# Spreading the rough score pieces of the first attention over other steps, in a macaron network on one Trainium2 core

## What is computed

```python
q, k, v = (heads(x @ W) for W in (Wq, Wk, Wv))       # 16 heads of 16
scores = jnp.einsum('bthd,bshd->bhts', q, k) * tril  # a later key counts as score 0
attn = softmax(scores / T ** 0.5)
out = jnp.einsum('bhts,bshd->bthd', attn, v) @ Wo
```

## Time and profile before

| | us |
|---|---|
| median of 3 runs | 2254.46 (2253.89 to 2258.62) |
| the profiled execution | 2254.67 |
| its span, first to last instruction | 2252.9 |
| TensorE busy in the span | 2004.6 (89%) |
| VectorE busy | 1301.1 (58%) |
| ScalarE busy | 785.7 |
| GpSimd busy | 866.8 |

### The profile page before, as it was taken

The page is one execution under the profiler, slowest core; times in us unless marked ns, Lnnn a source line. Parts: engine busy times, 40 slices in busy tenths (PEclk is TensorE's granted clock), DMA queues, the critical chain, the costliest instruction groups (busy, mean ns, idle before and its releaser), DMA issues. The chain is left out here.

```text
span 2252.9 us, 29291 instructions
## 1 busy us (share of the span) xinstructions
PE 2004.6 (89%) x8700; PEld 1245.8 (55%) x8701; DVE 1301.1 (58%) x2970; ACT 785.7 (35%) x1293; POOL 866.8 (38%) x684
## 2 busy tenths in 40 slices
PE   5899868889888799967599999999899999999987
PEld 5566635545554666646455555555565555555456
DVE  7322275777785722237466666666656666666525
ACT  1122244555555122223223333333413333433323
POOL 0344301231112044432026555556425555565632
PEclk9999969999999599988579999999999999999999
DMA  9111132331220811132331122122122222211101
GB/s 380 47 63 58 54 122 29 42 44 29 29 29 7 341 56 60 61 103 109 73 69 42 46 56 50 38 54 56 22 63 57 57 52 56 56 45 42 31 0 50
DMA packets 60569, 150.62 MB, mean 67 GB/s; under 512 B 12977, under 2 KB 18305, under 8 KB 58177
## 3 DMA queue, kind: packets, MB, share of 16 engines
q1 hardware_dynamic: 50208, 120.43, 20.4%
q0 software_dynamic: 9120, 24.92, 3.5%
q10 hardware_dynamic: 1152, 4.19, 0.5%
HBM read 68.95 MB, written 18.61 MB: 39 GB/s over the span
## 5 line engine op out<-in xcount | busy, mean ns | idle before, releaser
L1831 POOL TENSOR_TENSOR mla_PS<-mla_PS,mla_PT 128x1024 f32<-128x1024 f32 x192 | 457.7, 2384 | 222.2 <-ACT mla_PT L2110 219.6
L2253 DVE TENSOR_REDUCE mla_MXP<-PS 128x1 f32<-128x512 f32 x512 | 343.3, 689 | 241.9 <-PE PS L1910 236.6
L2110 ACT ACTIVATE mla_PT<-PS 128x1024 f32<-128x1024 f32 x256 | 262.4, 1026 | 401.9 <-PE PS L1929 399.5
L1938 PE MATMUL PS<-mla_PT,mla_CN 128*64 128x512 f32 x1024 | 275.3, 616 | 0.1
L1910 PE MATMUL PS<-mla_KH,mla_QH 113*128 113x512 f32 x512 | 216.6, 459 | 30.1 <-DMA mla_KL<-mla_SL 18.8
L521 DVE COPY moe_HT<-PS 128x512 f32<-128x512 f32 x92 | 63.6, 692 | 306.9 <-PE PS L644 301.0
L1929 PE MATMUL PS<-mla_QH,mla_KH 113*128 113x512 f32 x512 | 211.3, 413 | 1.0 <-ACT mla_QH L2097 1.0
L675 POOL DMA_INDIRECT moe_XS<-rows_in,moe_GI x96 | 93.5, 974 | 307.1 <-PE PS L630 171.7
L1929 PE MATMUL PS<-mla_QL,mla_KH 113*128 113x512 f32 x512 | 202.2, 395 | 0.0
L1929 PE MATMUL PS<-mla_QH,mla_KL 113*128 113x512 f32 x512 | 201.3, 393 | 0.0
L1910 PEld LDWEIGHTS PS<-mla_KH,mla_QH 113*128 113x128 f32 x512 | 90.7, 193 | 192.0 <-DVE mla_MXP L2253 123.5
(11 more groups left out here) (297 smaller groups left out, 3203.2 us busy)
## 6 DMA issues: line engine op xcount, KB each, us to landing
W<-in_W_dram SPq DMA_DIRECT2D x16, 2048.0 KB, 28.1
mla_QH<-mla_SH SPq DMA_DIRECT2D x64, 128.0 KB, 2.4
mla_KH<-mla_SH SPq DMA_DIRECT2D x64, 128.0 KB, 2.4
mla_QL<-mla_SL SPq DMA_DIRECT2D x64, 128.0 KB, 2.5
mla_KL<-mla_SL SPq DMA_DIRECT2D x64, 128.0 KB, 2.4
mla_KH<-mla_SH SPq DMA_DIRECT2D x64, 96.0 KB, 2.4
mla_KL<-mla_SL SPq DMA_DIRECT2D x64, 96.0 KB, 2.4
sums_Y<-rows_out SPq DMA_DIRECT2D x9, 512.0 KB, 6.1
```

The costliest lines, as they stand in the source:

```text
L1831: pool.tensor_tensor(PS[:, :], PT[:, slot(0), :] if k == 1 else PS[:, :], PT[:, slot(k), :], ALU.add).then_inc(s_ps.handle, 1)
L1938: ins = pe.matmul(bank(6)[h * DKVL:(h + 1) * DKVL, :], CN[:, b, k, 0:DKVL], PT[:, slot(k), h * HB:(h + 1) * HB], start=(k == 0), stop=(k = ...
L2110: act.activation(PT[:, slot(k), :], banks(st_bank(s, 0), 2)[:, :], ACT.Exp, scale=MLA_SCALE).then_inc(s_p.handle, 1)
L2253: dve.tensor_reduce(MXP[:, n // NPC, c, h, t:t + 1], bank(piece_bank(n))[:, :], AX_X, ALU.max).then_inc(s_mx.handle, 1)
```

## The change

It alters two tables. `per_slot` says how many rough pieces a slot does. Before: 2 in slots 8 to 11, 1 in slots 12 to 15, 2 in slots 16 to 23 and 2 in slots 0 to 5 of the next group. After: 2 in each slot from 8 to 23, 2 in slots 0 to 2, 1 in slots 3 and 4 and none in slot 5. So 32 pieces, not 28, are done by the end of slot 23, and before slot 0 of group 0. The assertion is loosened to match. `FILL` moves the filler of slot 6 to slot 7; every group has one there.

```diff
-    per_slot = {s: 2 for s in range(FROM, NSL)} | {s: 1 for s in range(FROM + 4, FROM + 8)} | {s: 2 for s in range(6)}
-    assert sum(per_slot.values()) == NPC and sum(per_slot[s] for s in range(FROM, FROM + 8)) == NPC0
+    per_slot = {s: 2 for s in range(FROM, NSL)} | {0: 2, 1: 2, 2: 2, 3: 1, 4: 1}
+    assert sum(per_slot.values()) == NPC and sum(per_slot[s] for s in range(FROM, FROM + 8)) >= NPC0
...
-    FILL = (3, 6, 9, 13, 15, 22)
+    FILL = (3, 7, 9, 13, 15, 22)
```

## The result

The changed kernel takes 2265.9 us (median of 5 runs, 2264.79 to 2267.84) against 2254.96 (5 runs) for the kernel before: a ratio of 1.0051, with a 95% interval of 1.0041 to 1.0062. It is slower by 10.9 us. The forecast was 2264. The profiled execution's span went from 2252.9 to 2264.6. Two single executions further down, one of the kernel before (2608 us, granted clock 0.73 in the mean) and one of the kernel with half of the clear moved (2863 us, 0.65), lie far above all others, whose mean clock is about 0.94, and are left out of every comparison.

What follows compares the result with a forecast made beforehand. TensorE, busy 89% of the span, was taken as the bound, so only its stops and clock could move. Terms +4.5, +6.3, +4.9 and -5.5 gave +10.2 us on 2254.67: 2264, slower by 0.4%; 8-in-10 range 2253 to 2273.

Steps and rivals of the forecast that it cites:

- Slots 3 to p0: Slots 3 to the start of p0: shorter, saving 4.0 us in groups 1 to 3 and 3.0 in groups 4 to 6.
- the second chain, VectorE's: VectorE's maxima, copies and first clear before p0: would allow p0 12.8 us after group 1's slot 0, against 13.3 by transfers.
- The stop at p12: Slot 14: TensorE waits for the second clear, 2.3 us in groups 1 to 3 and 2.9 in groups 4 to 6.
- The clock behind it: After the stop in slot 14, TensorE's clock falls to half, costing 1.8 us in each of groups 1 to 6.
- The clock around p0: Around p0: the old half-clock stretch may stay; if gone, worth 1.4 us in groups 4 to 6, half of it taken.
- the double fall: Rival: the clock is at half after p0 too, in every group, +8 us, 2272; chance 0.15.
- Opening and group 0: Before slot 0, four more pieces cost 2.9 us; group 0 gains nothing before p0 and loses later; together +4.9 us.
- Group 7: Last group, without p0, transfers or clear: slots 3 to 7 shorter, half clock in slots 8 and 9 gone; together -5.5 us.
- Slots 19 to 2: Slot 19 to slot 2 of the next group: pieces shift by four, no change, give or take 0.3 us a group.
- The sum: Whole kernel: +4.5 us groups 1 to 3, +6.3 groups 4 to 6, +4.9 opening and group 0, -5.5 group 7: +10.2.

## Why the prediction was right, step by step

- *Slots 3 to p0.* Right. The join's stop was expected at 0.2 and is gone, the filler's wait at 0.8 and is 0.76, p0 at 13.3 after slot 0 and is at 13.43 and 13.24, and it is the transfers that release it, 1.73 us late in group 5. There the clear ends at 614.99, 0.33 us before p0, so the second chain, VectorE's, was as close as counted; in group 3 it came last, and p0 stands at 13.80. The landing was hit with some luck: the last of the 12 transfers lands 7.4 us after its issue (410.41 to 417.82 in group 1) and p0 follows 0.04 later, where I had the median 7.1 and 0.3. In each burst the time to landing grows from 3.3 us for the first to 7.4 for the last, since SP issues one every 0.64 us and one lands every 1.0 us. So for this burst the wait is a backlog. The Trainium skill, "DMA: Bandwidth & Descriptors", section "Anatomy of one DMA — SWDGE (gpsimd) path", has a fixed 2.0 us plus bytes over 436 GB/s, an estimate of 2.3 us for these 128 KB. The trace agrees for other transfers of that size, which SP issues just as closely in the latent attention:

```profile
mla_QH<-mla_SH SPq DMA_DIRECT2D x64, 128.0 KB, 2.4
```

Why those of the first attention pass only at 1.0 us each, no run tried.
- *The stop at p12.* Right in kind and place, shown from both sides (the clear in slot 11, and in slot 16 of the old spread). Expected 2.3 us in groups 1 to 3 and 2.9 in 4 to 6, measured 1.88 and 2.52, 13.2 in six groups where 12 to 17 were given: 0.4 too much each time. Slots 12 to 18 were expected at 12.94 + 3.7 + 1.8 = 18.4 in group 1 and 19.0 in group 5; they are 18.24 and 18.69.
- *The clock behind it.* It falls in five of the six groups, not in group 3. Taken at 1.8, measured at 1.47 where it can be told apart. The half rule of "TensorE: Matmul & The Clock Gate" in the Trainium skill, section "Terms", would give an estimate of 1.7 for those 3.41 us, between the two.
- *The clock around p0.* This step failed. I let it go in half of the cases for groups 4 to 6 and let groups 1 to 3 have none after p0. But the filler's wait and p0's new stop (0.76 and 0.8 to 1.9 us) are still there, and the fall came behind p0 in groups 1 and 4 to 6. From p0 to slot 12 the change was expected at 0 in groups 1 to 3 and -0.7 in 4 to 6. It is +1.2 in group 1, -0.1 in 2 and 3, and +0.2, +1.3 and +1.2 in 4 to 6, in all 5.9 us more than forecast. That is a part of the double fall I had as a rival at 2272. Why the clock falls behind p0 in some groups and not in others stays open.
- *Opening and group 0.* Expected +4.9, measured 4.2 at the start of slot 0 plus 1.9 in group 0. In the opening four pieces add 2.9 us, as counted; what lies behind them, partly at half clock, takes 0.4 us more, and 0.95 is a later start of the whole part, which the change does not touch.
- *Group 7.* Expected -5.5, measured -6.5 up to its slot 22 (26.95 for 33.47): the clock does not fall at all, and slots 8 and 9 were worth more. They took 4.11 us at half clock, not the 4.94 of the earlier trace rows, which reach into slot 10, and now take 2.24: a gain of 1.9 where I had 1.0. After the change they and the next two slots run at full clock:

```profile
712.15:717.09 4.94, 4.94 (x35) 2.86 (x34) 0.85 (x2) 4.73 (x7) 1.77 (x4) 1.00 0.01 3
```

That is 35 matmuls in the time that held 23.
- *Slots 19 to 2.* Taken as nothing: 0.14 to 0.34 less in slots 19 to 23, 0.22 to 0.24 more in slots 0 to 2.
- *The sum.* Groups 1 to 3 were to lose 4.5 and lost 3.1 (group 3 without a fall even gained 0.4); groups 4 to 6 were to lose 6.3 and lost 9.6. With 6.1 for the opening and group 0 and -6.5 for group 7 it is 12.3, and the stages behind are 0.6 shorter: 11.7 in the profiled spans. My 10.2 on the profiled execution is 2264.7 by the median; I cut it to 2264. That the forecast came so close is in part luck. The way from p0 to slot 12 cost 5.9 us more than forecast, the opening and group 0 1.2 more, and slots 0 to p0 1.1 more. Against that slots 12 to 18 cost 3.4 less (in group 3 the clock did not fall), slots 19 to 23 1.6 less and group 7 1.0 less.

## What to carry to other kernels

When work is moved earlier in a hand-written schedule, ask for each piece what else it waits for beside its data: here a cheap memset that had stood two slots ahead of its only reader was overtaken, and 1.8 us of VectorE's time a group cost 17 us in six groups. And before paying for a shorter stretch, ask what is late next: p0 had a second bound in the transfers, so of the 4.4 to 5.0 us that slots 3 to 7 gave up in groups 1 to 6, 0.8 to 1.8 could not be used, and in group 0 nothing could. The parts of such a change should be timed alone: one half of it was a gain of 7 us, and the other hid that.

## What the runs showed of the hardware

How long TensorE stops in front of p12 does not decide by itself whether the clock falls behind it. Stops of 0.70 and 1.35 us (half of the clear moved, three groups each) were followed by no fall. Stops of 1.88 us went either way: the clock fell in groups 1 and 2 of the changed kernel and of the one with group 0 in the old spread, but in group 3 of neither, nor in groups 1 to 3 with the pieces alone. Stops of 2.52 us were followed by a fall each time, nine in those three kernels. Yet of three stops of 2.85 us in slot 16 of the old spread only one was. What else decides it no run shows. In group 1 such a fall cost 1.5 us on top of the stop.

A memset of one partition by 1024 elements takes GpSimd 0.95 us and VectorE 0.91, so either can make it, if its queue has the room. And where an instruction waits for two things, the profile may name the one that had come already: the times of both must be looked up, as at p0 of group 3.
